# Extra 128-row matmuls between the masked scores of the projection stage, and an earlier fetch of the first block's K and Q parts

## The reference

```python
qkv = layer_norm(x, g1, be1) @ w_qkv            # x: (4096, 128)
q, k, v = (qkv[:, 0], qkv[:, 1], qkv[:, 2])     # after reshape to (n, 3, 8, 16)
scores = jnp.einsum('nhd,mhd->hnm', q, k) * SCALE
scores = jnp.where((adj != 0)[None], scores, -jnp.inf)
attn = jax.nn.softmax(scores, axis=-1)
out = jnp.einsum('hnm,mhd->nhd', attn, v).reshape(n, DIM)
x = x + out @ w_proj + b_proj
x = x + jax.nn.gelu(layer_norm(x, g2, be2) @ w1 + b1) @ w2 + b2
```

## Time and profile before

| | us |
|---|---|
| median of three runs | 3419.3 |
| the profiled execution | 3420.85 |
| its span | 3419.0 |
| TensorE busy in the span | 3283.0 (96%) |
| VectorE busy | 2741.6 (80%) |
| projection stage, first layer, until its barrier | about 0 to 142.8 |
| projection stage, second layer, first scores to barrier | about 1787.6 to 1890 |

### The profile page before, as it was taken

One profiled execution on the slowest core, in us unless ns is written; L12 is line 12 of the kernel. 1 busy time (PEld: TensorE's weight loads), 2 busy tenths in 40 slices (PEclk: granted clock), 3 DMA queues, 4 the chain that ended last, 5 costly groups with the idle time before them and its releaser, 6 DMA issues.

```text
span 3419.0 us, 71092 instructions
## 1 busy us (share of the span) xinstructions
PE 3283.0 (96%) x22132; PEld 1440.7 (42%) x22152; DVE 2741.6 (80%) x8790; ACT 2430.8 (71%) x3557; POOL 2532.8 (74%) x1532
## 2 busy tenths in 40 slices
PE   7999999999999999999769999999999999999978
PEld 3434344443434343442544444444444444444326
DVE  6888888888989898980338899999999999999514
ACT  3379797978888797968322577777777777777753
POOL 3178878887878788889222588888888888888960
PEclk7599999999999999999886799999999999999989
DMA  8787887878787878774247656565656666565432
GB/s 232 202 274 231 274 257 247 270 237 279 233 287 223 293 217 289 246 249 140 81 112 177 178 153 198 158 187 167 184 170 183 173 180 176 177 177 175 146 90 72
DMA packets 502485, 683.05 MB, mean 200 GB/s; under 512 B 60896, under 2 KB 282464, under 8 KB 502112
## 3 DMA queue, kind: packets, MB, share of 16 engines
q1 hardware_dynamic: 501824, 678.40, 65.9%
q10 hardware_dynamic: 288, 0.10, 0.0%
HBM read 514.17 MB, written 164.10 MB: 198 GB/s over the span
## 4 chain that ended last, share of the span: by engine, by line
PE 85%; issue 5%; DVE 3%; DMA 2%; POOL 2%; SPq 1%; ACT 1%; POOLq 1%; DVEq 0%; ACTq 0%
PE PS L578 29%; PE PS L561 21%; PE PS L585 17%; PE PS L591 14%; DVE spill L931 2%; PE PS L506 1%; POOL arena L1121 1%; PE PS L639 1%; ACT arena L823 1%; DMA q_t<-max_dram 1%; PE PS L518 1%; POOLq L1083 1%; PE PS L709 0%; PE PS L511 0%; PE PS L498 0%
## 5 line engine op out<-in xcount | busy, mean ns | idle before, releaser
L931 DVE CUSTOM_DVE_ANT_0 spill<-PS,mask_n 128x512 bf16<-128x512 f32 x4096 | 2592.5, 687 | 331.8 <-PE PS L561 324.5
L823 ACT ACTIVATE arena<-PS 128x512 f32<-128x512 f32 (+1 forms) x3072 | 2133.6, 739 | 622.4 <-PE PS L585 376.5
L1121 POOL TENSOR_TENSOR arena<-arena,mask 128x1024 int32<-128x1024 int32 x896 | 2131.3, 2379 | 432.9 <-ACT arena L823 365.2
L561 PE MATMUL PS<-k_t,q_t 48*128 48x512 f32 x4096 | 1660.0, 536 | 27.7 <-issue 10.4
L585 PE MATMUL PS<-q_t,k_t 50*128 50x512 f32 x4096 | 1259.2, 485 | 14.8 <-DMA q_t<-max_dram 11.9
L591 PE MATMUL PS<-arena,idb 64*128 64x512 bf16 x4304 | 1152.9, 389 | 0.0
L578 PE MATMUL PS<-arena,v_sb 128*32 128x512 f32 x8192 | 1096.7, 607 | 8.1 <-POOL arena L1121 7.7
L561 PEld LDWEIGHTS PS<-k_t,q_t 48*128 48x128 f32 x4096 | 605.3, 193 | 961.5 <-DVE pmax L931 876.1
L585 PEld LDWEIGHTS PS<-q_t,k_t 50*128 50x128 f32 x4096 | 594.0, 188 | 188.1 <-issue 113.3
L591 PEld LDWEIGHTS PS<-arena,idb 64*128 64x128 bf16 x4304 | 311.9, 94 | 401.2 <-PE PS L591 255.6
L931 DVE DVE_READ_ACCUMULATOR2_ANT pmax<- 128x1 f32 x4096 | 340.0, 83 | 0.0
(11 more groups left out here) (56 smaller groups left out, 727.3 us busy)
## 6 DMA issues: line engine op xcount, KB each, us to landing
mask<-m_dram SPq DMA_DIRECT2D x768, 256.0 KB, 2.8
mask_n<-mn_dram SPq DMA_DIRECT2D x768, 128.0 KB, 2.9
adj_in<-in_adj SPq DMA_DIRECT2D x256, 256.0 KB, 4.4
mask<-in_adj_t SPq DMA_DIRECT2D x256, 256.0 KB, 4.1
m_dram<-mask SPq DMA_DIRECT2D x256, 256.0 KB, 3.7
mn_dram<-mask_n SPq DMA_DIRECT2D x256, 128.0 KB, 4.4
mt_dram<-arena SPq DMA_DIRECT2D x256, 128.0 KB, 3.6
arena<-mt_dram SPq DMA_DIRECT2D x256, 128.0 KB, 2.8
```

What stands on the lines that cost most here:

```text
L561: pe.matmul(ps_a[:, (L * NSC + n) % A_BANKS, :], q_t[r0:r0 + KROWS, gb % Q_SLOTS, pair, q * P:(q + 1) * P], k_t[r0:r0 + KROWS, pair, mb * ...
L823: nc.scalar.activation(p_buf[:, t % P_SLOTS, heads, :], ps_b[:, heads, :], ACT.Exp, scale=SCALE).then_inc(exped[part], 1)
L931: dve.tensor_tensor_reduce(spill[:, bank, :], ps_a[:, bank, :], mask_n[:, v % N_SLOTS, :], 1.0, LOWEST, ALU.subtract, ALU.max, pmax[:, p % ...
L1121: pool.tensor_tensor(p, p, m, ALU.mult).then_inc(p_masked, 1)
```

## The change

Two edits. First, `keep_busy` adds a float32 matmul of 128 rows, 128 columns and 512 moving columns (identity times `xn_t`) that writes PSUM bank 4, which nothing reads in this stage. There are three in each of the 8 blocks and one behind every fourth score of the tail, 8 there: 32 in a layer, 64 in all. Second, SyncE's list is reordered: block 0's K and Q loads move from 1.1 and 1.15 to 0.7 and 0.75, directly behind the stores; the feed-forward weights move from 0.7 to 3.3; adjacency pieces move from +0.1 to +0.76.

```diff
-                order += [(g + 1.1, "K", g) for g in range(NB)]
-                order.append((1.15, "Q", 0))
-                order.append((0.7, "f", L))
+                order += [(g + 1.1 if g > 0 else 0.7, "K", g) for g in range(NB)]
+                order.append((0.75, "Q", 0))
+                order.append((3.3, "f", L))
...
-                        order.append((v // NS + 0.25 * (v % NS) + 0.1, "a", v))
+                        order.append((v // NS + 0.25 * (v % NS) + 0.76, "a", v))
...
+            def keep_busy(gx):
+                pe.matmul(PS[:, 4, :], idf[:], xn_t[:, gx % 2, :], start=True, stop=True)
...
                     take_hi(gi, K)
                     score_two(2)
+                    keep_busy(gx)
                     take_hi(gi, Q)
...
                     score_two(5)
+                    keep_busy(gx)
                     score_two(6)
+                    keep_busy(gx)
                     score_two(7)
                 for n in range((NB - 2) * NS * 4, NB * NS * 4):
                     score_a(L, n)
+                    if n % 4 == 3:
+                        keep_busy(2 * L * NB + NB - 1)
```

## The result

The changed kernel is slower: 3443.82 us (median of four runs, 3438.66 to 3446.04) against 3418.36 us. The ratio is 1.0072, with a 95% interval of 1.006 to 1.0085. The forecast was 3399 us with a range of 3388 to 3413. The profiled execution took 3443.73 us, its span is 3441.9 us, against 3420.85 and 3419.0 before.

The account below looks back on a forecast made before the run. It took the projection stage to be held by TensorE's 0.50 clock and late row scores, with VectorE setting the tails' pace. -12.3 us (second layer) and -8 (first) made -20.3, a median of 3399 us, range 3388 to 3413.

Parts of the forecast that it names:

- additions of 128 rows lift the clock in the blocks: Projection stage: added 128-row matmuls bring the clock from 0.50 to 1.00 in blocks 3 to 7 and the tails.
- third rival: Blocks and tails: the clock isn't lifted, +90 us, about 3505 us; chance 0.03.
- The tail, the step that failed: Tail of each layer: at full clock each of 8 additions makes VectorE wait about 0.15 us, 1.2 us in all.
- first sign of being wrong: Tails: the forecast would be wrong if the clock there reads 0.50 instead of 1.00.
- second rival: Clock falls in the tail, or late adjacency pieces hold ScalarE; total -4 to -13 us, 3406 to 3415; chance 0.25.
- 6.8 us of VectorE's waits over six: Six blocks with scores: VectorE idles 0.9 us in each of four with statistics, some 1.6 in the other two.
- 93.6 us from the first reduction to the last: Each layer's projection stage after: 83.1 us of VectorE work plus waits of 6.8, 2.5 and 1.2 us.
- 7.8 and 9.2: Gain in us between first and last reduction, second and first layer, before start gains and the first layer's DMA limit.
- TensorE at 11.3 and VectorE at 11.0 us: A block at full clock with three additions: TensorE and VectorE come out nearly level, neither hiding all of the other.
- forecast 36: First layer's start: first score at 36 us, a gain of 2.4 us, bounds -5.9 and +3.
- 4.5 us sooner: Second layer's start: first score 4.5 us earlier as the feed-forward weights move behind the Q load; bounds 0 and 8.
- The DMA limit: First layer: queues at 96.4% of 16 engines hold the stage's end to 134 us, so at most 8 us come out.

Follow-up runs that it names:

- e6: The changed kernel with an addition after every second score of the tail, 16 instead of 8 a layer; 3420.1 us, ratio 1.0002 to before.
- e1: The changed kernel without the 8 additions in each layer's tail, block additions and new order kept; 3411.2 us, ratio 0.9981 to before.
- e7: The changed kernel without tail additions and with the adjacency pieces at their old place; 3408.2 us, ratio 0.9965 to before.
- e9: e7 with three more additions ahead of block 2's first score; 3409.7 us, ratio 0.9965 to before.
- e11: e7 without the additions in blocks 0 and 1, which have no scores; 3410.7 us, ratio 0.997 to before.
- e5: The changed kernel without the three additions in each block, tail additions and new order kept; 3448.5 us, ratio 1.0088 to before.
- e2: The changed kernel without any additions, only SyncE's new order kept; 3418.6 us, ratio 1.0002 to before.
- e3: The changed kernel with all additions but SyncE's order as before; 3443.8 us, ratio 1.0068 to before.
- e8: e7 with two additions in a block instead of three, the last one gone; 3428.9 us, ratio 1.0028 to before.

## Why the prediction was wrong

**The clock.** That additions of 128 rows lift the clock in the blocks was right: their mean is 0.92 and 0.88, from 0.66 and 0.69. The third rival, by which busy time alone counts, didn't happen. The rule of the Trainium skill ("TensorE: Matmul & The Clock Gate", Part 1) that the clock follows how busy the engine is doesn't tell these tails apart: busy 98% of the time at 0.50 before, which speaks against it, and 99% at 1.00 in e6, which agrees.

**The tail, the step that failed.** The prediction wrote "each addition makes VectorE wait about 0.15 us: 8 x 0.15 = 1.2 us". It assumed a clock of 1.00, and credited the three banks as 1.83 us of work in hand. Both were wrong. VectorE has about 1.05 us of work left when the addition starts, for the fourth score ahead of it had itself waited for a bank. Even at 1.00 the group takes 2.87 us, a wait of 0.43 instead of 0.15, and at 0.50 it is 4.42, a wait of 1.98. The tail at 0.50 was the first sign of being wrong that the prediction named. The clock fell after one group in the first layer and after two in the second, and stayed down. The second rival had this fall, with a price of 3.44 us a group against 2.44; it counted TensorE's own work and left out that the fourth score waits for a reduction in series with it. With 4.42, for 13 groups, it would have come to +26 us against the forecast, 3425 and not 3406 to 3415. e1 shows that taking the eight out gives 33 us back, 23.4 of it seen in the two tails. Forecast and profiled execution differ by 43.2 us (-20.3 against +22.9), so the tails are about half of the miss; the blocks and the starts, which gave less than forecast, make most of the rest.

**The blocks.** Forecast were 11.9 us a block with statistics, and 6.8 us of VectorE's waits over six. In the changed kernel, blocks without statistics take 11.8 us (96.4 to 108.2), those with them 12.9 (56.1 to 69.0), and in each layer one takes 14.5 to 15.4 in which the clock falls once. The forecast had 93.6 us from the first reduction to the last, which is some 95.2 as counted in the tables here (first score to the end of the last reduction, 103.0 us before in the second layer); e7, the best case, has 98.4 to 98.5, and e1 102.7 and 102.8. That leaves a gain of 0.2 to 1.6 us a layer in e1 and some 5 in e7, instead of 7.8 and 9.2. e7's trace is of its fastest run; e9 and e11, whose blocks with scores have the same additions, have 100.0 to 103.1. The blocks of e5, without any addition in them, took 66.0 and 68.2 us, those of e2, as bare, 68.3 and 70.6; beside that spread the gain of e7's 65.7 and 65.6 is small. By the medians, the additions in the blocks are worth 7.5 us in both layers together (e1's 3411.2 against e2's 3418.6). The term was mis-sized. TensorE at 11.3 and VectorE at 11.0 us were level only on paper, and each fall of the clock in a block, which cost 1.6 and 2.5 us (14.5 and 15.4 against 12.9), was left out.

**The starts.** First layer: forecast 36, measured 41.3. The piece that "is issued behind the Q load, at some 26 us" was issued at 25.91, just so; but ScalarE got it only at 35.18. e7, with pieces ahead, has 35.4. Second layer: 4.5 us sooner were forecast, 1.2 were measured, and e3 has 1.3 with the old order. The Q load, forecast to be issued about 1 us earlier at best, was issued 14.8 us behind the first transpose instead of 13.7. Why the first score waits as long behind it as it does stays open.

**The DMA limit** of the first layer was not what decided. In e7 its last reduction is at 133.9 us, near the 134 that the share of 96.4% gave, but the second layer, which has no such share, took as long (98.4 against 98.5 us). It isn't shown to bind.

Of the 22.9 us, the two tails make 19.7, the later first score 2.8 (less 1.2 in the second layer), the blocks -2.4, the stretch between the layers -0.5. The rest, 4.5 us behind the last reduction of the second layer's projection stage, stays open. Nearly all of it, 4.3 us, lies behind the last reduction of that layer's attention stage (209.4 us to the end against 205.1; the other traces have 205.2 to 207.4), where the two programs are the same; by then the delay at the barrier had been made up.

## What to carry to other kernels

An addition that is to raise the clock must be priced at the low clock as well, and with everything that stands in series with it: with few buffers a matmul in an in-order queue costs its own time plus the round trip that refills them. Where another engine sets the pace, as in these tails, a faster clock gave nothing by itself, and filler lost at either clock. Take filler out stage by stage before judging the idea: here one part lost about 33 us and the rest, with the better load order, gained about 11.

## What the runs showed that I had not expected

More filler can be faster: 16 additions a tail gave 3420.1 us, 8 gave 3443.8 (and none 3411.2). Fewer can be slower: two in a block instead of three cost 20.6 us (e8 against e7).

The same instructions need not take the same time. e1 and e7 have the same program in the second layer's projection stage, and it took 102.8 us in one profile and 98.4 in the other: in one, a block of 14.5 us in which the clock fell, and a longer first block, in the other neither. Runs of e1 spread from 3407.4 to 3421.6 us, so a few us between two of these kernels are not told apart by one trace. The stages that no kernel here changes vary too: from the first layer's last reduction to the second's first transpose the traces have 1610.8 (e3) to 1622.6 us (e4).
